# Graph layer on one core: edge lists in two halves, one-hots on VectorE alone, layer norm woven into the first product

## The reference, cut to what matters

```
xn = layernorm(x)
x  = x + gnn(xn, src, dst) + attention(xn)       # linear attention, 16 heads of 64
x  = x + moe(layernorm(x))                       # 8 experts, top 2, and a shared expert

gnn:  h   = relu(xn @ W_self0 + mean(xn) @ W_neigh0 + b0)
      out = h @ W_self1 + mean(h) @ W_neigh1 + b1
mean(h)[n] = sum over edges with dst == n of h[src], divided by max(degree of n, 1)
```

## Time and profile before

| what | value |
|---|---|
| runs | 1252.89, 1253.34, 1256.2 us; median 1253.34 |
| profiled execution | 1256.77 us, its span 1255.0 us |
| mean granted clock of PE | 0.97 of full |
| PE matmul busy | 1155.9 us (92%), 6601 instructions |
| PE weight load busy | 1007.4 us (80%) |
| DVE busy | 567.7 us (45%) |
| ACT busy | 375.5 us (30%) |
| POOL busy | 382.4 us (30%) |

### The profile page before, as it was taken

One profiled execution on the slowest core, in us unless ns is written; L12 is line 12 of the kernel. 1 busy time (PEld: TensorE's weight loads), 2 busy tenths in 40 slices (PEclk: granted clock), 3 DMA queues, 4 the chain that ended last, 5 costly groups with the idle time before them and its releaser, 6 DMA issues.

```text
span 1255.0 us, 17030 instructions
## 1 busy us (share of the span) xinstructions
PE 1155.9 (92%) x6601; PEld 1007.4 (80%) x6601; DVE 567.7 (45%) x837; ACT 375.5 (30%) x425; POOL 382.4 (30%) x449
## 2 busy tenths in 40 slices
PE   3699999996786899999999999999999999999993
PEld 2579988674564699988788999888998998998982
DVE  6722245543666554131245342425445545545533
ACT  3323322320101012030132422225544544544510
POOL 3277777787999610000000051200000000000031
PEclk9799999997898899999999999999999999999997
DMA  6122211251201011061100533365576576576553
GB/s 224 67 68 68 69 35 34 62 192 52 83 1 68 1 67 68 3 230 67 67 1 34 184 69 138 122 245 198 203 267 210 191 267 222 181 266 233 176 211 127
DMA packets 85686, 159.14 MB, mean 127 GB/s; under 512 B 15558, under 2 KB 15862, under 8 KB 85632
## 3 DMA queue, kind: packets, MB, share of 16 engines
q1 hardware_dynamic: 64908, 127.30, 29.4%
q0 software_dynamic: 12976, 14.91, 3.8%
q10 hardware_dynamic: 7748, 16.19, 3.4%
HBM read 136.85 MB, written 21.51 MB: 126 GB/s over the span
## 4 chain that ended last, share of the span: by engine, by line
PE 61%; POOL 16%; issue 7%; DVE 7%; DMA 3%; DVEq 3%; POOLq 1%; ACT 1%; SPq 0%; ACTq 0%
PE ps L1438 20%; PE ps L1440 20%; PE ps L1439 20%; POOL edges_by_bin L550 13%; DMA y_second<-expert_rows,slots 2%; DVE dst_oh L1198 2%; DVEq L1208 1%; DVE w_lo L924 1%; POOL src_oh L569 1%; DVE c_f L1209 1%; PE ps L1477 1%; DMA w_raw<-in_L_mix_Wv 1%; DVEq L1199 1%; ACT w_hi L660 1%; POOLq L570 1%
## 5 line engine op out<-in xcount | busy, mean ns | idle before, releaser
L924 DVE TENSOR_TENSOR w_lo<-w_raw,w_hi 128x2048 fp32r<-128x2048 f32 x108 | 243.1, 2289 | 176.5 <-ACT w_hi L660 175.7
L660 ACT CAST w_hi<-w_raw 128x2048 fp32r<-128x2048 f32 x108 | 201.8, 1910 | 158.4 <-PE ps L1440 65.3
L550 POOL DMA_INDIRECT edges_by_bin<-list_v,list_at x157 | 170.3, 1085 | 68.0 <-issue 49.0
L1440 PE MATMUL ps<-xe_hi,w_lo 128*128 128x256 f32 x512 | 144.9, 283 | 0.0
L1439 PE MATMUL ps<-xe_lo,w_hi 128*128 128x256 f32 x512 | 144.9, 283 | 0.0
L1438 PE MATMUL ps<-xe_hi,w_hi 128*128 128x256 f32 x512 | 144.9, 283 | 0.0
L569 POOL TENSOR_SCALAR src_oh<-iota_n,src_f 128x128 f16<-128x128 f16 x196 | 128.2, 670 | 12.8 <-issue 9.8
L1438 PE MATMUL ps<-w_hi,xt_hi 128*128 128x512 f32 (+1 forms) x240 | 101.4, 423 | 0.0
L1438 PE MATMUL ps<-w_hi,he_hi 128*128 128x512 f32 x256 | 101.0, 395 | 0.0
L622 POOL COPY idx<-cols 128x2 uint32 x8 | 3.6, 446 | 316.0 <-DVE xe_lo L930 316.0
L1439 PE MATMUL ps<-w_lo,he_hi 128*128 128x512 f32 x256 | 99.8, 390 | 0.0
(11 more groups left out here) (278 smaller groups left out, 2213.3 us busy)
## 6 DMA issues: line engine op xcount, KB each, us to landing
w_raw<-in_L_ffn_w SPq DMA_DIRECT2D x64, 1024.0 KB, 5.2
w_raw<-in_L_gnn_W_neigh SPq DMA_DIRECT2D x8, 1024.0 KB, 5.1
w_raw<-in_L_gnn_W_self SPq DMA_DIRECT2D x8, 1024.0 KB, 5.0
w_raw<-in_L_ffn_shared_gate_up SPq DMA_DIRECT2D x8, 1024.0 KB, 5.9
expert_rows<-y_s ACTq DMA_DIRECT2D x32, 256.0 KB, 5.3
w_raw<-in_L_mix_Wv SPq DMA_DIRECT2D x4, 1024.0 KB, 7.8
w_raw<-in_L_mix_Wk SPq DMA_DIRECT2D x4, 1024.0 KB, 4.9
w_raw<-in_L_mix_Wq SPq DMA_DIRECT2D x4, 1024.0 KB, 5.0
```

The lines of the kernel that those rows point to most:

```text
L550: nc.gpsimd.indirect_dma_start(out=list_d, out_offset=bass.IndirectOffsetOnAxis(ap=list_at[0:P, c:c + 1], axis=0), in_=list_v[0:P, c:c + 1 ...
L660: copy(w_hi[b][:, s * HK:(s + 1) * HK, :], w_raw[s][:, :, :]).then_inc(hi_done, 1)
L924: V_.tensor_tensor(w_lo[b][:, k, :], w_raw[s][:, :, :], as32(w_hi[b][:, k, :]), ALU.subtract).then_inc(lo_done, 1)
L1440: return mat(out_ap, ll, rh, start=False, stop=stop)
```

## The change

- **Two lists.** The chunks are cut into list 0 (80 chunks) and list 1 (77), each with its own bins, at most 29 groups each: 58 groups in all, each a unit `cnt` of its own. SP loads list 0 in its queue behind the two bias loads and ahead of the second half of Wo; POOL loads list 1 when its scatters are done.
- **One-hots by DVE alone.** Both one-hots of a group are one `tensor_tensor` each on f16 data, the four chunks interleaved (innermost dimension of 4 elements), three groups ahead. POOL makes none. PE reads its operands at a step of 4 elements (8 bytes).
- **Counts spread.** Groups of list 0 stand behind the second to the tenth O product (4, 4, then 3 each), those of list 1 behind all ten neighbour projections (3 each, the last 2).
- **Sorting.** Bin marks and the add and mask move from POOL to DVE; scan, ranks and places come later in DVE's program.
- **Layer norm in PE's order.** PE transposes tile i + 1 in the middle of v(0, i), after the first 4 of 8 row blocks, and waits for the two quarters of Wv one by one. ACT normalises tile 0 ahead of the first cast of weights.
- **End.** The ten gathers move 128 rows in the last tile too, where they moved 113.

```diff
-    MAXG = (E + BINS * (GE - 1)) // GE
-    LC = MAXG * GC
-    CU = -(-MAXG // 2)
-    GBUF = 4
-    BATCH = 16
+    LISTS, BATCH = 2, 16
+    LW = -(-NC // (LISTS * BATCH)) * BATCH
+    NP = LISTS * LW
+    MAXG = (LW * 128 + BINS * (GE - 1)) // GE
+    CU = LISTS * MAXG
+    LC = CU * GC
+    GBUF = 3
...
-    units = [("xt", 0), ("xt", 1), ("v", 0, 0), ("xt", 2), ("rank",), ("v", 0, 1)]
-    for i in range(2, NT):
-        units += ([("xt", i + 1)] if i + 1 < NT else []) + [("v", 0, i)]
+    units = [("xt", 0)]
+    for i in range(NT):
+        units += [("v", 0, i)] + ([("xt", i + 1)] if i + 1 < NT else []) + ([("rank",)] if i == NT - 2 else [])
...
+                    for turn in range(2):
+                        sp.wait_ge(edges_stored[turn], 16 * stored_by(0, turn))
+                    sp.dma_start(list_i[:, 0:MAXG * GC], list_of(0)).then_inc(list_loaded[0], 16)
...
-                        out=y_g[c][0:R(i), i, :], out_offset=None, in_=y_d,
-                        in_offset=bass.IndirectOffsetOnAxis(ap=slots[0:R(i), c, i:i + 1], axis=0)).then_inc(yg_loaded[i][c], 16)
+                        out=y_g[c][:, i, :], out_offset=None, in_=y_d,
+                        in_offset=bass.IndirectOffsetOnAxis(ap=slots[:, c, i:i + 1], axis=0)).then_inc(yg_loaded[i][c], 16)
...
             root(0)
+            normal(0)
             split_hi(J_V, quarters=(0,))
-            normal(0)
+            normal_hi(0)
+            root(1)
             split_hi(J_V, quarters=(1,))
-            root(1)
-            normal_hi(0)
             normal(1)
...
+            def one_hots(g):
+
+                b, of_group = g % GBUF, slice(g * GC, (g + 1) * GC)
+                V_.tensor_tensor(dst_oh[b][:, :, :], iota_n[:, :, :],
+                                 dst16[:, of_group].unsqueeze(1).to_broadcast([128, TH, GC]), ALU.is_equal)
+                V_.tensor_tensor(src_oh[b][:, :, :], iota_n[:, 0:128, :],
+                                 src16[:, of_group].unsqueeze(1).to_broadcast([128, 128, GC]), ALU.is_equal)
+                V_.drain().then_inc(oh_ready, 1)
...
+                for k in range(KF):
+                    if k % HK == 0:
+                        pe.wait_ge(lo_out, nth[("xt", i, k // HK)])
+                        pe.wait_ge(lo_done, 2 * b + k // HK + 1)
+                    last = passes(PB(key)[0:R(i), :], [t[:, k, tile(i)] for t in XT],
+                                  (w_hi[b][:, k, :], w_lo[b][:, k, :]), k == 0, k == KF - 1)
+                    if h == 0 and k == HK - 1 and i + 1 < NT:
+                        normal_first(i + 1)
+                        if i + 1 == NT - 1:
+                            ranks()
```

More of the change, by code:

```diff
@@ L103, in gps_layer @@
         mixed.append(key)
-        last = CU if m == len(mains) - 1 else min(CU, 2 * (m - FIRST_CNT + 1))
-        while u < last:
+        t = m // FIRST_CNT[1]
+        left = (t + 1) * MAXG - u
+        tiles_left = (t + 1) * FIRST_CNT[1] - m
+        for _ in range(-(-left // tiles_left) if m >= FIRST_CNT[0] else 0):
             mixed.append(("cnt", u))
             u += 1
+    assert u == CU
     units += mixed
@@ L159, in gps_layer @@
     FULL = (NT - 1) * T
+    list_of = lambda t: list_d.rearrange("(p c) o -> p (c o)", p=128)[:, t * MAXG * GC:(t + 1) * MAXG * GC]
+    stored_by = lambda t, turn: sum((c - t * LW) // BATCH % 2 == turn for c in range(t * LW, min((t + 1) * LW, NC)))
     def in_pieces(t, a):
@@ L254, in following @@
             return t
[L256 to L264, removed]
@@ L534, in _ @@
             nc.gpsimd.memset(ctx_s[:, :, :], 0.0)
-            nc.gpsimd.iota(iota_n[:, :], [[1, TH]], base=0, channel_multiplier=0, allow_small_or_imprecise_dtypes=True)
+            nc.gpsimd.iota(iota_n[:, :, :], [[1, TH], [0, GC]], base=0, channel_multiplier=0, allow_small_or_imprecise_dtypes=True)
             nc.gpsimd.drain().then_inc(pads_set, 1)
[L538 to L552, removed]
             pool.wait_ge(ready[slot(("xt", NT - 1))], use(("xt", NT - 1)) + 1)
@@ L555, in _ @@
             nc.gpsimd.drain().then_inc(c_cleared, 1)
-            pool.wait_ge(ready[slot(("at", KF - 1))], use(("at", KF - 1)) + 1)
[L557 to L566, removed]
-                for c in range(GC):
-                    e = g * GC + c
-                    nc.gpsimd.tensor_scalar(src_oh[:, b + c, :], iota_n[:, 0:128], src_f[:, e:e + 1], None, ALU.is_equal)
-                nc.gpsimd.drain().then_inc(src_ready, 1)
+            pool.wait_ge(none_stored, 16)
+            for t in range(LISTS):
+                pool.wait_ge(list_at_ready, t + 1)
+                for c in range(t * LW, min((t + 1) * LW, NC)):
+                    P = 128 if c < EVENC else EDGES
+                    lap, turn = divmod((c - t * LW) // BATCH, 2)
+                    if lap and c % BATCH == 0:
+                        pool.wait_ge(edges_stored[2 * t + turn], 16 * BATCH * lap)
+                    nc.gpsimd.indirect_dma_start(
+                        out=list_d, out_offset=bass.IndirectOffsetOnAxis(ap=list_at[0:P, c:c + 1], axis=0),
+                        in_=list_v[0:P, c:c + 1], in_offset=None).then_inc(edges_stored[2 * t + turn], 16)
+            for turn in range(2):
+                pool.wait_ge(edges_stored[2 + turn], 16 * stored_by(1, turn))
+            pool.wait_ge(ready[slot(("at", KF - 1))], use(("at", KF - 1)) + 1)
+            pool.dma_start(list_i[:, MAXG * GC:LC], list_of(1)).then_inc(list_loaded[1], 16)
             pool.wait_ge(cnt_done, CU)
@@ L1009, in firsts @@
                 V_.drain()
-                V_.tensor_tensor_scan(grp_end[:, :], ones_b[:, :], grp[:, :], 0.0, ALU.mult, ALU.add)
+                for t in range(LISTS):
+                    of_list = slice(t * BINS, (t + 1) * BINS)
+                    V_.tensor_tensor_scan(grp_end[:, of_list], ones_b[:, :], grp[:, of_list], float(t * MAXG), ALU.mult, ALU.add)
                 V_.drain()
@@ L1225, in _ @@
                 (attention_out if key[0] == "o" else neighbour_lo)(*key[1:])
-                if key == mains[FIRST_CNT]:
-                    edge_list()
-                    one_hots(0)
-                    one_hots(1)
+                if mains.index(key) in FIRST_CNT:
+                    t = FIRST_CNT.index(mains.index(key))
+                    edge_list(t)
+                    for g in range(GBUF):
+                        one_hots(t * MAXG + g)
             wait_unit(("deg",))
@@ L1481, in values @@
                 key = ("v", h, i)
-                weights(J_V + h)
-                pe.wait_ge(lo_out, nth[("xt", i, 1)])
+                b = J_V + h
                 claim(key)
-                by_tokens(key, PB(key)[0:R(i), :], XT, J_V + h, tile(i)).then_inc(ready[slot(key)], 1)
+                for k in range(KF):
[8 more added lines that the diff above has]
+                            ranks()
+                last.then_inc(ready[slot(key)], 1)
             def across(key, source, i):
@@ L1511, in count @@
                 claim(key)
[L1512 to L1517 removed]
+                b = u % GBUF
+                pe.wait_ge(oh_ready, u + 1)
+                for c in range(GC):
+                    last = mat(PB(key)[:, 0:TH], src_oh[b][:, :, c], dst_oh[b][:, :, c], start=c == 0, stop=c == GC - 1)
                 last.then_inc(ready[slot(key)], 1)
```

211 lines of the change are left out of this document (108 added, 103 removed).

## The result

| | before | after |
|---|---|---|
| median of the runs, us | 1254.62 (1252.89 to 1256.2, 4 runs) | 1244.19 (1243.16 to 1244.43, 4 runs) |
| ratio of the times | | 0.9916, 95% interval 0.9898 to 0.9933 |
| profiled execution, span, us | 1256.77, 1255.0 | 1243.16, 1241.3 |
| mean granted clock of PE | 0.970 | 0.983 |

The kernel is faster by 0.8%, about half of what was forecast (1233). I follow the three forecast places, and then what lies between them.

A forecast was written before the change was run, and what follows sets the result against it. PE was taken as fully busy except in the opening, the counts and the end; -16.6 - 16 + 12 = -20.6 gave a span of 1234.4 and a time of 1232.7, say 1233, with 1220 to 1256 for 8 in 10.

The forecast's parts named there:

- the three forecast places: The opening, the counts and the end, where PE is not fully busy; only these were priced.
- The end, -16.6: After PE's last matmul: last gathers of 128 rows land after 6.9 us, DVE ends at 1235.4, not 1251.98; -16.6 us.
- The opening, -16: Up to v(1, 0): first product near 17.3, then 39.2 us of PE's work, v(1, 0) at 57; -16 us.
- the bound of -18: Opening: the largest gain allowed for; the smallest was -5.
- The counts, +10 and 2 for the clock: Count stage: DVE alone needs 188.5 us and ends at 450.0, not 440.04; 2 us more for PE's clock.
- X: Counts: DVE's time for a group's two one-hots, taken as 1.14 us, between 0.67 and 2.06.
- the period: Counts: DVE's time for one group, 0.83 + 0.48 + 0.26 + X, 2.71 us where it was 2.5.
- The 0.85 per main product: Counts: DVE's time for each of 18 main products, 0.85 us, together 15.3.
- The base: Whole kernel: the old profiled execution's difference from the runs' median was applied to span 1234.4, giving 1232.7.
- The rivals that were named: Five: slow one-hots (0.10), PE bounding counts (0.08), smaller opening gain (0.06), long gathers (0.04), list 1 late (0.02).
- the rival by which the opening gains only 5: Opening: waits and low clock return, so it gains only 5 us; 1244, chance 0.06.
- the second rival's bound: Counts: PE stays hidden up to 1.13 us a group, even if 0.585 doubles; trebled gives 1269, chance 0.08.

The follow-up runs named there:

- rows128_only: The kernel before with only the ten last gathers moving 128 rows in the fifth tile too; 1236.46 us, ratio 0.9856.
- opening_only: The kernel before with the new order of layer norm and products, but one list, sorted by POOL as before; 1259.83 us, ratio 1.0034.

## Why the prediction fell short

- **The end, -16.6:** right (-16.6; in rows128_only the span ends 3.6 behind PE's last matmul, too). The gathers land a little later than assumed (`y_second` after a median of 8.3 us, at most 9.3, for 6.9), which costs nothing.
- **The opening, -16:** right in size (-15.6), but by errors that cancel, which is luck. The first product came 3.2 us late, behind the held operation of DVE, and the waits between the tiles were 2.6 us where 0.5 had been added. Against this PE's own work up to v(1, 0) took 34.4 us and not 39.2, because less of it ran slowly. opening_only, where nothing holds DVE, gains 19.4 in this stage, more than the bound of -18. And that the gain reaches the end only because the counts no longer wait for the whole list, the prediction has in half a sentence ("list 0 is long loaded") while it prices the opening as a gain of its own; opening_only shows the condition.
- **The counts, +10 and 2 for the clock:** 12 forecast, 9.7 found. X, the period and list 1 (needed at 342, loaded by 284 and not 320) were right or on the safe side. DVE begins at 244.2 and not at 245.5, and needs 189.9 us where 188.5 and 2 had been added. The 0.85 per main product does not come out of the rows named for it (8.88 us, less 3.74 for additions and one-hots and 4.49 for the subtraction, is 0.65); about 1.0 was found, waits included. The scatters beside DVE's one-hots took 0.95 to 1.5 us and not 2.46.
- **The step that failed** is the sentence of the first part, "Everything else is PE's and the change leaves it as it is, so only these three places are priced". Behind the last addition stand four sums and four drains of POOL, on the path. The prediction moved the clearing of `c_f` ahead of the scatters at no cost, and did not ask what its drain had been paying: 4.42 us of "issue" stood behind it in the profile of before, in front of the list's load. With it gone, the first drain after the scatters is the one among the sums. It costs +8.7 us between the last addition and `deg_s` (the gap of 7.86 and 1.1 for `deg` at the lower clock, less 0.3), and three runs take the gap off the path, each in another way.
- **The base.** I subtracted 1.7 us for the difference between the profiled span and the median, as if it belonged to every kernel. But a run's time is 1.8 to 1.9 us more than its own span, in both kernels; the sign came from an old profiled execution that was a long one. The changed kernel's was the shortest of four, and its median lies 2.9 above its profiled span. The 29 spans of the kernel before in the experiments' runs go from 1250.3 to 1255.7, the four of the changed kernel from 1241.3 to 1242.6. What makes the old ones vary is known only in part (rows128_only).

Together: 8.7, less 1.9 for the counts and the opening, is 6.8 of the 6.9 us by which the span passes 1234.4; with 2.9 and 1.7 for the base that is the distance of 11.5 from 1232.7 to 1244.19. The rivals that were named all fell: none of them was about POOL after its scatters. The measured 1244 is the number of the rival by which the opening gains only 5, but by chance, since the opening gained 15.6. The count matmuls did double, and stayed hidden as the second rival's bound allowed.

## What to carry to other kernels

When a change moves the first operation and drain behind a row of indirect DMAs, look for the "issue" gap behind it in the profile of before, and ask which drain comes first afterwards; put one there on purpose, where nobody waits. Price every instruction between the last stage that changes and the next thing that PE waits for, on whatever engine it is. And do not take the difference between one profiled execution and a median over to a changed kernel unless you know the stage that causes it.

## What the runs showed of the hardware

- The first drain of POOL behind indirect scatters takes 5 us after 8 of them, 6.5 to 7.0 after about 80, and 7.9 after 157, even 150 us later; later drains have no such gap. With a memset of 2.73 us directly behind the scatters 4.4 are left.
- A DVE operation with one source in SBUF (int32 to f32, 160 elements) lasted 4.3 us, to the end of POOL's iota, and 1.6 when the iota was elsewhere, to the end of POOL's memset.
- At a granted clock of 1.00, twelve count matmuls of 314 f16 columns take 3.53 us when both operands are read at a step of 8 bytes, and 1.80 when contiguous; at 0.50 to 0.52 they take 3.83 and 3.76.
- After 9.4 us without work PE ran the four `deg` matmuls in 2.46 us at a granted clock of 0.50; after 2.1 us without work in 1.33 at 1.00.
- DVE's `tensor_tensor` on f16 does 1256 elements in 0.81 us when both operands have four neighbouring elements innermost, and in 1.47 with an innermost step of 0 in one of them.
